# The last chunk's key norms: Newton steps moved from VectorE to GpSimd in three pieces, and the work of the chunk before moved in beside them

## The reference

```python
k, v, q = x @ W_k.T, x @ W_v.T, x @ W_q.T      # each in 32 blocks of 8
def step(S, kvq):                              # S: 32 blocks of 8 x 8
    k_norm = k_t / (norm(k_t, axis=-1) + 1e-06)
    retrieved = einsum('bnij,bnj->bni', S, k_norm)
    S_new = tanh(S + einsum('bni,bnj->bnij', v_t - retrieved, k_norm))
    Sq = einsum('bnij,bnj->bni', S_new, q_t)
    return S_new, Sq * silu(Sq)
```

## Time and profile before

| | us |
|---|---|
| median of 3 runs | 1164.92 (1164.45 to 1167.81) |
| the profiled execution | 1167.29 |
| its span | 1165.4 |
| `finish()` on VectorE in it, from the end of its last small row on | 1066.5 to 1162.9 |

### The profile page before, as it was taken

The page is one execution under the profiler, slowest core; times in us unless marked ns, Lnnn a source line. Parts: engine busy times, 40 slices in busy tenths (PEclk is TensorE's granted clock), DMA queues, the critical chain, the costliest instruction groups (busy, mean ns, idle before and its releaser), DMA issues.

```text
span 1165.4 us, 16455 instructions
## 1 busy us (share of the span) xinstructions
PE 1082.1 (93%) x5761; PEld 835.7 (72%) x5761; DVE 962.4 (83%) x1401; ACT 606.6 (52%) x1039; POOL 484.3 (42%) x379
## 2 busy tenths in 40 slices
PE   6999999999999999999999999999999999997154
PEld 3666666677787777788778787877888787785043
DVE  3688888883035998999899899989988998999895
ACT  2344555554435356645745564475457456553555
POOL 1366767775333244433424432442443244331321
PEclk9999999999999999999999999999999999998677
DMA  6334544763531440523134043313413331330001
GB/s 233 127 134 157 184 168 178 274 224 92 178 109 47 137 125 19 143 75 127 55 110 155 24 125 87 120 51 106 132 64 108 90 108 45 119 91 1 0 1 39
DMA packets 45339, 127.02 MB, mean 109 GB/s; under 512 B 4320, under 2 KB 21472, under 8 KB 43104
## 3 DMA queue, kind: packets, MB, share of 16 engines
q1 hardware_dynamic: 44416, 114.72, 31.1%
q10 hardware_dynamic: 864, 11.54, 2.6%
HBM read 117.86 MB, written 19.92 MB: 118 GB/s over the span
## 4 chain that ended last, share of the span: by engine, by line
DVE 56%; PE 26%; issue 9%; ACT 6%; POOL 2%; DMA 1%; DVEq 0%; ACTq 0%; SPq 0%; POOLq 0%
DVE tmp L2046 7%; PE lower L441 7%; PE lower L1167 6%; DVE tmp L2036 6%; DVE Sq L2038 5%; DVE tmp L2052 5%; DVE delta L2048 4%; PE bank L1167 4%; PE lower L541 2%; DVE stats L142 2%; DVE delta L2050 2%; DVE S L2054 2%; DVE newton L214 1%; ACT look L646 1%; DVE whole L1998 1%
## 5 line engine op out<-in xcount | busy, mean ns | idle before, releaser
L1861 POOL TENSOR_TENSOR a_lo<-whole,a_hi 128x512 fp32r<-128x512 f32 x128 | 182.0, 1439 | 268.3 <-ACT a_hi L1484 197.1
L1167 PE MATMUL lower<-b_hi,ring 128*128 128x512 f32 x512 | 193.7, 396 | 1.4 <-ACT a_hi L1484 1.4
L1167 PE MATMUL lower<-b_lo,ring 128*128 128x512 f32 x512 | 190.6, 390 | 1.7 <-POOL b_lo L1861 1.7
L1167 PE MATMUL lower<-a_hi,ring 128*128 128x512 f32 x496 | 186.4, 394 | 1.7 <-issue 1.7
L1167 PE MATMUL lower<-a_lo,ring 128*128 128x512 f32 x496 | 184.2, 390 | 0.2 <-POOL a_lo L1861 0.2
L1861 POOL TENSOR_TENSOR b_lo<-whole,b_hi 128x512 fp32r<-128x512 f32 x64 | 93.4, 1467 | 145.5 <-ACT b_hi L1484 145.5
L1467 ACT ACTIVATE S<-S 128x1024 f32<-128x1024 f32 x56 | 58.6, 1059 | 183.0 <-DVE S L2054 183.0
L1483 ACT ACTIVATE whole<-lower,hs 128x512 f32<-128x512 f32 x126 | 86.2, 684 | 76.8 <-PE lower L1167 76.7
L441 PE MATMUL lower<-wa,xT 128*128 128x512 f32 x240 | 111.2, 607 | 10.4 <-DMA wa<-wa_dram 7.4
L1167 PEld LDWEIGHTS lower<-b_hi,ring 128*128 128x128 f32 x512 | 96.2, 188 | 22.0 <-issue 1.8
L1167 PEld LDWEIGHTS lower<-b_lo,ring 128*128 128x128 f32 x512 | 96.0, 188 | 22.0 <-POOL b_lo L1861 2.3
(11 more groups left out here) (275 smaller groups left out, 2350.4 us busy)
## 6 DMA issues: line engine op xcount, KB each, us to landing
ring<-ffn_copy_dram SPq DMA_DIRECT2D x128, 512.0 KB, 3.6
look<-ffn_dram ACTq DMA_DIRECT2D x6, 1879.0 KB, 7.0
ffn_copy_dram<-ffn_dram SPq DMA_DIRECT2D x8, 1408.0 KB, 9.5
xT<-xT_dram SPq DMA_DIRECT2D x8, 512.0 KB, 8.4
rope<-rope_dram SPq DMA_DIRECT2D x8, 512.0 KB, 8.1
xtok<-x_dram SPq DMA_DIRECT2D x8, 512.0 KB, 4.5
x1in<-x_dram SPq DMA_DIRECT2D x8, 512.0 KB, 4.8
x1res<-x_dram SPq DMA_DIRECT2D x8, 512.0 KB, 3.3
```

What stands on the lines that cost most here:

```text
L1167: ins = nc.tensor.matmul(out, a, b, start=(first and n == 0), stop=(last and n == len(pairs) - 1))
L1861: nc.gpsimd.tensor_tensor(lo[:, m, :], t["whole"][:, m % 4, :], hi[:, m, :].bitcast(F32), ALU.subtract).then_inc(lo_done, 1)
```

## The change

What it does:

- The 9 Newton operations, the multiplication and the addition of 1e-6 leave VectorE. `guess_of` keeps the sum and the bit guess there, GpSimd's `key_root` makes 13 operations (each waits for the one before it), and `scaled_keys` takes the reciprocal and scales the keys on VectorE. There are three pieces: row 0, row 1, and rows 2 and 3.
- VectorE's order changes: both halves of `earlier_x3` stand at the front, and `earlier_gate` behind `first_state`.
- The product of the state with the query for row 3, half 0 moves from VectorE to GpSimd (`read_q(3, 0)`), and `read_sum(2, 0)` stands ahead of `next_state(2, 1)`.
- Turned rows lie in banks 0 to 3, those of the down product, in place of two banks used in turn; TensorE begins row 1's keys when row 1 is turned and not when all are. Queries have bank 5, and ScalarE's copies of them stand later in its order.
- Some semaphores are joined (two of the attention's are one now), without a change in order.

```diff
                     def turn_row(b):
                         pe.wait_ge(fin_x2, b + 1)
-                        if b >= 2:
-                            pe.wait_ge(fin_turned, b - 1)
...
-                    def scan_row(b):
...
-                        pe.wait_ge(fin_turned, BATCH if b else 1)
...
+                    def key_value_row(b):
+
+                        pe.wait_ge(fin_turned, b + 1)
+                        if b >= 2:
+                            pe.wait_ge(fin_kvq, 2 * (b - 2) + 1)
...
+                    def query_row(b):
+
+                        if b:
+                            pe.wait_ge(fin_kvq, 2 * b)
...
+                    def key_root(n, rows):
+
+                        x, y, z = (t[a][:, rows].rearrange("p b n -> p (b n)") for a in ("norm", "root", "newton"))
+                        steps = Steps(pool, norm_root, NORM_STEPS)
+                        steps.begin(n)
+                        pool.wait_ge(norm_guess, n + 1)
+                        for last in (False, False, True):
+                            w = x if last else y
+                            if last:
+                                steps.wait()
+                                steps.done(nc.gpsimd.tensor_tensor(x, x, y, ALU.mult))
+                            steps.wait()
+                            steps.done(nc.gpsimd.tensor_tensor(z, w, y, ALU.mult))
+                            if not last:
+                                steps.wait()
+                                steps.done(nc.gpsimd.tensor_tensor(z, z, x, ALU.mult))
+                            steps.wait()
+                            steps.done(nc.gpsimd.tensor_scalar(z, z, -0.5, 1.5, ALU.mult, ALU.add))
+                            steps.wait()
+                            steps.done(nc.gpsimd.tensor_tensor(w, w, z, ALU.mult))
+                        steps.wait()
+                        steps.done(nc.gpsimd.tensor_scalar(x, x, 1.0, 1e-6, ALU.mult, ALU.add))
+                        steps.end()
...
                     x2_root(1, slice(1, BATCH))
+                    key_root(0, slice(0, 1))
+                    key_root(1, slice(1, 2))
+                    added_mean(0, every)
                     read_q(0, 0)
-                    added_mean(0, every)
                     added_root(0, every, t["rstd4"], t["shift4"])
+                    key_root(2, slice(2, BATCH))
                     read_q(0, 1)
                     read_q(1, 0)
                     read_q(1, 1)
                     read_q(2, 0)
+                    read_q(3, 0)
                     added_mean(1, front)
                     read_q(2, 1)
...
-                    norms_of(slice(0, 1))
+                    earlier_x3(0)
+                    guess_of(slice(0, 1))
+                    earlier_x3(1)
+                    guess_of(slice(1, 2))
+                    scaled_keys(0, slice(0, 1))
+                    dve.wait_ge(fin_turned, BATCH)
                     first_state()
-                    earlier_x3()
-                    norms_of(slice(1, BATCH))
                     earlier_gate()
+                    scaled_keys(1, slice(1, 2))
                     next_state(0, 0)
+                    guess_of(slice(2, BATCH))
                     next_state(0, 1)
+                    scaled_keys(2, slice(2, BATCH))
                     read_sums(0)
...
                     gate_rows(front, 2, 1)
+                    read_sum(2, 0)
                     next_state(2, 1)
                     mixed_pair(1, 1)
-                    read_sums(2)
-                    last_read(0)
+                    read_sum(2, 1)
+                    read_sum(3, 0)
                     last_read(1)
```

More of the change, by code:

```diff
@@ L1049, in last_state, with turned_at @@
                     "p (n i j) -> p n i j", i=BS, j=BS)
+            KEY_BANK = (4, 6, 4, 6)
+            def turned_at(b):
+                return bank[b][:, 0:DIM]
+            NORM_STEPS = 13
             def fin_sums(t):
@@ L1401, in finish @@
                     turn_row(0)
-                    scan_row(0)
+                    key_value_row(0)
+                    query_row(0)
                     for b in range(1, BATCH):
@@ L1405, in finish @@
                     for b in range(1, BATCH):
-                        scan_row(b)
+                        key_value_row(b)
+                        query_row(b)
                     for g in range(2):
@@ L1757, in finish @@
                     nc.scalar.activation(tmpf[:, half_cols:], sqf, ACT.Square).then_inc(sq_tanh, 1)
+                    query_row(1)
+                    state_tanh(0, 0)
+                    key_value_row(2)
+                    state_tanh(0, 1)
+                    query_row(2)
+                    key_value_row(3)
+                    query_row(3)
                     add_rows(0, x3, range(BATCH), ln3_steps, d * N_LN3 + 2)
@@ L2180, in ffn_row, with guess_of @@
                         row_stats(fin, x2, range(b, b + 1))
-                    def norms_of(rows):
-                        n = rows.stop - rows.start
-                        x, y, z = (t[a][:, rows].rearrange("p b n -> p (b n)") for a in ("norm", "root", "newton"))
+                    def guess_of(rows):
+                        x, y = (t[a][:, rows].rearrange("p b n -> p (b n)") for a in ("norm", "root"))
                         dve.wait_ge(fin_ksq, rows.stop)
@@ L2238, in last_read, with earlier_x3 @@
                         nc.vector.tensor_reduce(sq_cols(s, hf), w, AX_X, ALU.add).then_inc(fin_sq, 1)
-                    def earlier_x3():
-                        tail.begin(d)
-                        for hf in range(2):
-                            read_out(d, BATCH - 1, hf, tail)
+                    def earlier_x3(hf):
+                        if hf == 0:
+                            tail.begin(d)
+                        read_out(d, BATCH - 1, hf, tail)
                     def earlier_gate():
```

93 lines of the change are left out of this document (50 added, 43 removed).

## The result

The changed kernel took **1169.84 us** (median of 20 runs, 1167.19 to 1178.91), the kernel before on the same chip 1166.73 (1164.45 to 1167.90, 20 runs): ratio **1.0033**, 95% interval 1.0024 to 1.0042, or 3.9 us slower by the ratio and 3.1 by the two medians. The profiled executions are closer together: 1168.09 us (span 1166.3) against 1167.29 (span 1165.4), +0.8. The forecast of +0.7 fits the profiles and not the medians, and most of the experiments are about that gap.

A forecast was written before the change was run, and what follows sets the result against it. VectorE was taken to bound the last 100 us, ScalarE 0.5 us behind. The lead of 6.4 us shrinks to 1.3, then the gate comes 0.7 us later: 1164.92 + 0.7 = 1165.6 us, range 1159.3 to 1171.

The forecast's parts named there:

- the forecast's own range: Whole kernel: gain and loss within 3.5 us of each other, 1162.8 to 1168.4 us; chance 0.50.
- rival (b): GpSimd's small steps cost more: 0.45 and 0.60 us each give +6, or 1171 us; chance 0.22.
- What a step costs: GpSimd's norm steps, 13 in a row: 0.33 us each for one row, 0.40 for two.
- Who holds whom: VectorE instructions with two SBUF inputs and GpSimd instructions reading SBUF exclude each other; the first to start holds the port.
- Rival (a): GpSimd's small steps and VectorE hardly hold each other: gate 5.6 us sooner, 1159.3 us; chance 0.28.
- Step 1: VectorE up to the first next_state: next_state(0, 0) at 1083.7 instead of 1090.14, 6.4 us ahead.
- the two waits (3.48 us): VectorE's pauses of 1.33 and 2.15 us for ScalarE's squared keys, counted in the 10.3 us at stake.
- Step 2: VectorE up to next_state(1, 0): 5.1 us added, so 1101.6 against 1102.92, 1.3 us ahead.
- Step 3: Up to chunk 7's gate: GpSimd's queue makes ScalarE 1.1 us later; gate at 1142.9 against 1142.18, 0.7 us later.

The follow-up runs named there:

- the read is kept back: Changed kernel with read_q(0, 1) kept back on GpSimd until VectorE's 128x512 key multiplication is over: 1169.87 us, ratio 1.0033.
- the kernel before with early fillers: Kernel before plus unused TensorE products, four ahead of the last chunk's down product and four ahead of row 0's turn: 1165.14 us, ratio 0.9987.
- its run with late ones: Kernel before plus five unused TensorE products in the last 30 us (three behind pair 2's turn, two behind its values): 1165.73 us, ratio 0.9998.
- restoring the reads: Changed kernel with early and late unused products, read_q(3, 0) taken out, last reads as in the kernel before: 1167.79 us, ratio 1.0016.
- the two kernels with fillers: Kernel before with unused products ahead of the rows, 1165.14 us; changed kernel with those and nine in the tail, 1168.70 us.
- the repeat: Changed kernel run once more, unchanged: 1170.05 us, ratio 1.0040 to the kernel before.
- the run with early fillers: Changed kernel plus unused TensorE products ahead of the last chunk's down product and row 0's turn: 1170.11 us, ratio 1.0027.
- the read moved without and with them: Changed kernel with read_q(3, 0) behind pair 2's root: 1167.71 us; with read_q(0, 1) also held and nine tail products: 1168.04 us.

## Why the prediction was right, and where it was off

**The range and the verdict's side.** 1169.84 lies in the range (to 1171), and the ratio of 1.0033 with its interval straddles the bound between no change and slower. The likeliest value was 4.2 us too low. Of that, 1.8 is the kernel before itself, whose median was 1166.73 and not 1164.92; 2.4 is the difference, +3.1 for +0.7. The time lies above the forecast's own range (to 1168.4), and only the upper bound of rival (b), whose dearer steps didn't come, takes it in: that much is luck. (As a difference, +3.1 lies inside the 3.5 us that the forecast gave itself, the 3.9 of the ratio outside.) So is part of the agreement of +0.7 with the +0.8 of the two profiles: the profile of the kernel before has a low clock at the keys, that of the changed kernel a high one at pair 3.

**What a step costs.** Forecast 0.33 and 0.40 us; measured 0.325 for 32 norms (1071.06 to 1074.64, 11 steps) and 0.38 for 64 (1091.57 to 1095.75, 11 steps). Rival (b) falls: VectorE's steps start every 0.226 us in the run that gave them back to it (1074.22 to 1076.48, ten of them), so GpSimd takes 1.44 times as long. The Trainium skill, "GPSIMD Engine Reference", section "Engine selection", has it at about 2 times; at this size the measurement decides against that.

**Who holds whom.** Shown as forecast: five steps of piece 1 at 0.49 to 1.20 us, the first steps of pieces 0 and 2 at 1.15 and 1.20, the multiplication at 2.35 us and 0.69 once the read is kept back. Rival (a) falls, and the Trainium skill's rule ("SBUF — State Buffer", section "Who interferes with whom") agrees with these rows. One hold was missed: L1913, the root of rows 1 to 3, took 1.78 us at 1066.69 (forecast as before, 0.86), because the read of chunk 6 now lies beside it.

**Step 1** forecast `next_state(0, 0)` at 1083.7, measured 1083.80. As a gain on the kernel before, 6.3 us, it holds for the profile of the earlier trace rows, which has a low clock at the keys. At an equal, higher clock it is 3.6 (1088.00 to 1084.38), of which 0.25 lies ahead of `finish()`'s part here (the last small row ends at 1067.44 and 1067.19). **This is the term that was mis-sized:** "with the two waits (3.48 us), 10.3 us of VectorE's time are at stake". 3.14 of those 3.48 us (all but 0.34) weren't there in the kernel before with early fillers, nor was the 2.15 in its run with late ones; they came with a granted clock of 0.65 at 1064 to 1068 and 0.57 at 1072 to 1076, while TensorE made the keys. `next_state(0, 0)` came only 2.14 us earlier in that kernel (1088.00 for 1090.14), since its last small row ended 0.95 later: the 1.0 us by which the first wait is shorter is spent ahead of it. The profiled execution was 2.4 us above the median of the three runs shown, and I carried the difference over to that median as it was, where I should have asked which of its waits made it slow. With 20 runs it is 0.6 above the median, so this term covers the smaller part of the 2.4 us by which the difference was missed; the larger part, 1.8, is that the changed kernel's usual execution is slower than its profiled one, for which see the clock at pair 3.

**Step 2** forecast a loss of 5.1 us, measured 4.68 (17.46 for 12.78). Guess 1.05 (forecast 1.2), wait 0.56 (0.9), reciprocal and undisturbed multiplication 1.3 (1.25), hold 1.66 (1.7).

**Step 3** forecast a loss of 2.0 us (from 1.3 ahead to 0.7 behind); measured 2.14 in the profile and 2.15 taken back at the gate by restoring the reads. `read_q(3, 0)` ended at 1129.86 (forecast 1130.2), ScalarE scaled at 1134.25 (1134.4), the gate came at 1142.66 (1142.9).

**The sum at equal clock** is therefore -3.6 + 4.7 + 2.15 = +3.2, and the gates of the two kernels with fillers stand 3.23 apart (3.48 counted from the end of the last small row). Seen the other way: VectorE is spared 6.86 us (2.47, 3.17, 1.22) ahead of the gate, waits or is held for 9.74 there (0.97, 0.92, 2.39, 0.55, 1.66, 1.15, 2.10; the kernel before 0.34), and what is left of the 3.48, 0.9 us, goes to the sums, shifts, reciprocals and gaps of three pieces in place of two.

**Not foreseen: the clock at pair 3.** In the changed kernel, the eight executions of 20 with a mean granted clock of 0.976 or more took 1167.2 to 1169.3 us, the eleven at 0.973 or 0.974 1169.3 to 1172.0 (one at 0.928 took 1178.9). The profile was one of the first kind; two profiles of the second kind (the repeat, and the run with early fillers) have the clock fall in pair 3's stretch after TensorE's pauses, which costs 1.5 and 1.6 us of wait. Nine fillers there gave 1.8 us, and nothing where the read had been moved; five gave nothing in the kernel before. That a shifted pause lets the clock fall is what these four runs (late fillers in either kernel, the read moved without and with them) suggest together. It isn't shown: which pause does it was not separated, and the one right ahead of pair 3 is longer in the profile in which the clock stays up.

No version of the change beats the kernel before. The kernel before itself with early fillers has a ratio of 0.9987 (0.9978 to 0.9996), a small gain in one set of runs.

## What to carry to other kernels

Before a wait in a profile is counted as time to be won, look at the granted clock of the engine that it waits for and at the profiled time beside the median of many runs: here 3.1 us of 3.5 us of waits were there only with the clock at 0.57 to 0.65, and without them `next_state(0, 0)` came 2.1 us sooner. Work taken off the busiest engine pays only as far as what it hands over comes back in time: VectorE lost 6.9 us of work and gained 9.4 us of waits and holds, as each handed-over piece was waited for right behind it. And an operation that is moved onto a queue has to be priced by what stands behind it there; the multiplication moved to GpSimd saved 1.22 us on VectorE, and with it the gate came 2.15 us later.

## What the hardware showed that I had not expected

- A GpSimd step of 32 norms and a 1.23 us VectorE instruction with two SBUF inputs took strict turns here: one step between any two, each about as long as its neighbour (1.10 to 1.20 us for 0.22 to 0.25).
- Unused products made a program faster: nine of them in the tail took the changed kernel from 1170.05 to 1168.21 us; five of them left the kernel before where it was (0.9998).
- TensorE's clock in the same code differs between executions: 0.57 or 1.00 at 1072 to 1076 in the kernel before and in the same code with fillers only later on; 0.75 or 1.00 at 1150 to 1155 in two executions of the changed kernel.
